# A two-iteration mixture stage: the state is kept as mu - x, and VectorE makes all picked rows

## What is computed

```python
v = zeros_like(xf); integrated = xf
for _ in range(2):
    ctx = concatenate([integrated, v], axis=-1)
    shared_ctrl = gelu(ctx @ shared_w1 + shared_b1) @ shared_w2 + shared_b2
    ctrl = experts(ctx, flat_idx, ...)            # two of eight experts a row, chosen once
    # for each of the three controls a, b, g = split(ctrl, 3):
    v_next = sigmoid(a) * v - softplus(b) * (x - mu)
    x_next = x + 0.1 * sigmoid(g) * v_next
    # weighted by sw, (1 - sw) * flat_w, and then by a halting share
    integrated = integrated + halt * (x_mix - integrated)
    v = v + halt * (v_mix - v)
refined = gelu(integrated @ refine_w1 + refine_b1) @ refine_w2 + refine_b2
out = xf + integration_weight * refined
```

## Time and profile before

| | |
|---|---|
| median of 3 runs | 3231.7 us (3231.43 to 3236.0) |
| the profiled execution | 3206.04 us |
| its span | 3204.3 us |
| PE busy | 2711.0 us (85%) |
| DVE busy | 2364.4 us (74%) |
| ACT busy | 1991.2 us (62%) |
| POOL busy | 1108.0 us (35%) |
| granted PE clock, mean | 0.897 |

### The profile page before, as it was taken

The page is one execution under the profiler, slowest core; times in us unless marked ns, Lnnn a source line. Parts: engine busy times, 40 slices in busy tenths (PEclk is TensorE's granted clock), DMA queues, the critical chain, the costliest instruction groups (busy, mean ns, idle before and its releaser), DMA issues. The chain is left out here.

```text
span 3204.3 us, 43614 instructions
## 1 busy us (share of the span) xinstructions
PE 2711.0 (85%) x16128; PEld 1864.2 (58%) x16128; DVE 2364.4 (74%) x3852; ACT 1991.2 (62%) x2961; POOL 1108.0 (35%) x824
## 2 busy tenths in 40 slices
PE   3989999898989907889888888988898889896986
PEld 2333333333333306777687767777786778685876
DVE  4577676677776736877887788778877887776998
ACT  1676676666667706666667666766676667664432
POOL 2112112021111114443445344434443444442776
PEclk8798898989899958989999899989898999898998
DMA  4352542516335030000000000000000000003231
GB/s 110 61 83 72 88 82 74 83 60 96 73 67 90 27 97 1 1 14 14 1 14 14 8 7 14 14 7 7 14 14 1 14 14 7 1 8 116 80 99 53
DMA packets 124789, 136.09 MB, mean 42 GB/s; under 512 B 16754, under 2 KB 104818, under 8 KB 124580
## 3 DMA queue, kind: packets, MB, share of 16 engines
q1 hardware_dynamic: 124580, 133.31, 18.4%
HBM read 86.87 MB, written 46.40 MB: 42 GB/s over the span
## 5 line engine op out<-in xcount | busy, mean ns | idle before, releaser
L380 ACT ACTIVATE probs<-psum_a 128x1024 f32<-128x1024 f32 (+3 forms) x768 | 604.3, 816 | 341.9 <-PE psum_a L643 337.9
L1410 PE MATMUL psum_f<-w,picked 128*128 128x256 f32 (+1 forms) x2304 | 722.4, 346 | 0.0
L1409 PE MATMUL psum_f<-w,picked 128*128 128x256 f32 x2304 | 626.3, 289 | 2.7 <-DVE picked L1238 2.7
L1410 PEld LDWEIGHTS psum_f<-w,picked 128*128 128x128 f32 x2304 | 452.2, 196 | 52.7
L975 POOL TENSOR_TENSOR picked<-hid,masks 128x512 fp32r<-128x512 f32 x256 | 347.0, 1365 | 368.7 <-PE psum_f L1410 326.5
L1409 PEld LDWEIGHTS psum_f<-w,picked 128*128 128x128 f32 x2304 | 456.7, 198 | 2.9 <-DVE picked L1238 2.9
L456 DVE TENSOR_SCALAR probs<-probs 128x2048 f32<-128x2048 f32 (+3 forms) x320 | 301.5, 942 | 192.4 <-ACT probs L380 192.4
L643 PE MATMUL psum_a<-q_stack,k_stack 72*128 72x512 f16 (+3 forms) x1536 | 399.3, 352 | 34.9 <-DMA q_stack<-q_rope_scratch 17.6
L1067 ACT ACTIVATE gates<-psum_f 128x256 f32<-128x256 f32 (+1 forms) x384 | 186.6, 492 | 302.4 <-PE psum_f L1410 278.7
L658 PE MATMUL psum_a<-probs,v 128*17 128x512 f32 (+3 forms) x3072 | 347.7, 527 | 1.8 <-DVE probs L456 1.7
L1238 DVE TENSOR_TENSOR picked<-hid,masks 128x512 fp32r<-128x512 f32 x256 | 228.6, 921 | 148.1 <-PE psum_f L1410 145.0
(11 more groups left out here) (284 smaller groups left out, 6096.2 us busy)
## 6 DMA issues: line engine op xcount, KB each, us to landing
heads_scratch<-kq_parts SPq DMA_DIRECT2D x64, 256.0 KB
k_stack<-heads_scratch SPq DMA_DIRECT2D x96, 128.0 KB
q_stack<-heads_scratch SPq DMA_DIRECT2D x96, 128.0 KB
x_in<-x_dram SPq DMA_DIRECT2D x8, 1024.0 KB, 5.3
x_res<-x_dram SPq DMA_DIRECT2D x16, 512.0 KB, 5.2
x_scratch<-y SPq DMA_DIRECT2D x16, 512.0 KB, 3.1
xs<-x_scratch SPq DMA_DIRECT2D x16, 512.0 KB, 3.9
xf_scratch<-xs SPq DMA_DIRECT2D x16, 512.0 KB, 2.9
```

The source lines that it names most:

```text
L380: act.activation(probs[:, s % PROB_SETS, 2 * u:2 * u + 2, q0:512], psum[:, 2 * u:2 * u + 2, q0:512], ACT.Exp, scale=exp_scale).then_inc(ex ...
L1409: pe.matmul(soft_out, x, cols[:, 1], start=start, stop=stop)
L1410: return pe.matmul(gate_out, x, cols[:, 2] if it == 0 else cols[:, 0::2], start=start, stop=stop)
```

## The change

1. The state in `xs` is mu - x from the normalisation on. `x_normalize` gets one more DVE operation over the block, x_minus_mu and its semaphore go from POOL, and `integrate` uses the state directly. The transposed state is negated where it is read out (ACT by a scale of -1, DVE by a multiplication by -1), and mu's share of each first layer, `W1^T mu`, is added to the biases once: 12 tiny matmuls and two additions at the start of `mixture`, 8 and one at the start of `refine`, with two more small loads of mu in each.
2. The iteration-0 update has 7 DVE instructions instead of 10; `tmp` gives way to `terms`, which holds both sums side by side.
3. The moments and the normalisation of a new block are made half a block earlier: behind the updates of units 2 and 3 of the "first" group of the block before.
4. DVE makes the lower picked rows as well (`pick`).
5. Of the ten mask spreads, DVE reads the five odd ones (`spread_rows`), ahead of its update of unit 2; and spread 1 goes from the fills of unit 1 to those of unit 2.

```diff
-                [("HT", k, 0, 0), ("H", k, 0, 0), ("H", k, 0, 1), ("MT", k, 0, 0), ("SP", k, 0, 0), ("SP", k, 0, 1)],
-                [("H", k, 0, 2)] + [("SP", k, 0, i) for i in range(2, 10)]]
+                [("HT", k, 0, 0), ("H", k, 0, 0), ("H", k, 0, 1), ("MT", k, 0, 0), ("SP", k, 0, 0)],
+                [("H", k, 0, 2)] + [("SP", k, 0, i) for i in range(1, 10)]]
...
     def on_act(job):
-        return job[0] in ("XT", "RT", "H", "LG", "HT") or job[0] == "SP"
+        return job[0] in ("XT", "RT", "H", "LG", "HT") or job[0] == "SP" and job[3] % 2 == 0
...
-            def pick_lower(n):
...
-            def x_minus_mu(n):
...
-                if t == 2 and kind == "second" and k + 2 < BLOCKS:
-                    x_scale(k + 2)
...
+                if t == 3 and kind == "first" and k + 1 < BLOCKS:
+                    x_scale(k + 1)
+                for job in hidden_jobs:
+                    lower_parts(job)
...
-                    act.activation(ctx_t[:, 0, i], src, ACT.Copy).then_inc(act_read, 1)
+                    act.activation(ctx_t[:, 0, i], src, ACT.Copy, scale=-1.0 if i < 2 else 1.0).then_inc(act_read, 1)
...
+            dve.wait_ge(mu_part, 1)
+            dve.tensor_tensor(b1[:], b1[:], psum[:, 0, 0:5], ALU.add)
+            after(dve.tensor_tensor(br1[:], br1[:], psum[0:HIDDEN, 0, 5:6], ALU.add))
...
-                last.then_inc(xn_ready, 1)
+                then_wait(last)
+                dve.tensor_tensor(xs[:, k % XS], mu[:].unsqueeze(1).to_broadcast([P, BT, D]), xs[:, k % XS],
+                                  ALU.subtract).then_inc(xn_ready, 1)
...
+            def spread_rows(k, places):
+
+                for i in places:
+                    job = ("SP", k, 0, i)
+                    job_ready(dve, job)
+                    s, place = divmod(i, 5)
+                    dve.tensor_copy(masks[:, k % MASKS, s, place], bank(job), saturate=False).then_inc(dve_read, 1)
...
                 for s in range(2):
                     if n >= 2:
                         dve.wait_ge(slot_done, SLOTS * (n - 2) + s + 2)
...
+                    for part, done in ((0, upper_picked), (1, lower_picked)):
+                        if (t, s, part) == (0, 0, 1):
+                            dve.wait_ge(lower_made, lower_value[("H", k, it, FULL - 1)])
+                        first = part if s == 0 else 1 - part
+                        dve.tensor_tensor(picked[:, n % 2, s, part], hid[:, hid_set(k, it), part, first:first + 4, tile_of(t)].bitcast(F32),
+                                          masks[:, k % MASKS, s, first:first + 4, tile_of(t)], ALU.mult).then_inc(done, 1)
...
                 if it == 0:
+                    then_wait(dve.tensor_tensor(q, sp_b, c.unsqueeze(2).to_broadcast([P, SLOTS, D]), ALU.mult))
+                    then_wait(dve.scalar_tensor_tensor(out=r, in0=tg, scalar=1.0, in1=q, op0=ALU.add, op1=ALU.mult))
                     for s in (1, 2):
+                        then_wait(dve.tensor_tensor(terms[:, 0], terms[:, 0], terms[:, s], ALU.add))
+                    dve.tensor_tensor(v, q[:, 0], z, ALU.mult)
+                    then_wait(dve.scalar_tensor_tensor(out=r[:, 0], in0=r[:, 0], scalar=-HALF_STEP, in1=z, op0=ALU.mult, op1=ALU.mult))
+                    dve.tensor_tensor(z, z, r[:, 0], ALU.add).then_inc(unit_done, 1)
...
+                if t == 2 and kind == "first":
+                    spread_rows(k, (1, 3, 5, 7, 9))
                 if t == 2:
                     integrate(n)
                 if n + 2 < UNITS:
-                    pick_upper(n + 2)
+                    pick(n + 2)
...
+                    if t == 2 and k + 1 < BLOCKS:
+                        x_row_stats(k + 1)
+                    if t == 3 and k + 1 < BLOCKS:
+                        x_normalize(k + 1)
                 if kind == "second":
                     if t == 1:
                         shared_lower(k, 1)
-                        if k + 2 < BLOCKS:
-                            x_row_stats(k + 2)
                     if t == 2:
                         coefficients(k, 1)
-                        if k + 2 < BLOCKS:
-                            x_normalize(k + 2)
...
+            pe.wait_ge(weights_in, 16 * len(loads))
+            for m in range(MC):
+                for c in range(2):
+                    last = pe.matmul(psum[:, 0, m:m + 1], raw_f1[:, c, P * m:P * m + P], mu_col[:, c:c + 1], start=(c == 0), stop=(c == 1))
```

More of the change, by code:

```diff
@@ L747, in on_act @@
     def on_act(job):
[L748 removed]
+        return job[0] in ("XT", "RT", "H", "LG", "HT") or job[0] == "SP" and job[3] % 2 == 0
     def on_dve(job):
[L751 removed]
+        return job[0] in ("XT", "MT") or job[0] == "SP" and job[3] % 2 == 1
     act_value = {job: n + 1 for n, job in enumerate([job for job in jobs if on_act(job)])}
@@ L1171, in x_lower @@
                 act_took(dve, job)
-                dve.tensor_tensor(ctx_t[:, 1, c], bank(job), ctx_t[:, 0, c].bitcast(F32), ALU.subtract).then_inc(dve_read, 1)
+                dve.scalar_tensor_tensor(out=ctx_t[:, 1, c], in0=bank(job), scalar=-1.0 if c < 2 else 1.0,
+                                         in1=ctx_t[:, 0, c].bitcast(F32), op0=ALU.mult, op1=ALU.subtract).then_inc(dve_read, 1)
             def shared_lower(k, it):
@@ L1274, in integrate @@
                     for s in range(SLOTS):
-                        last = dve.scalar_tensor_tensor(out=x, in0=tmp[:, s], scalar=d[s], in1=x, op0=ALU.mult, op1=ALU.add)
+                        last = dve.scalar_tensor_tensor(out=z, in0=q[:, s], scalar=d[s], in1=z, op0=ALU.mult, op1=ALU.add)
                         if s < SLOTS - 1:
@@ L1292, in _ @@
                 x_lower(1, 0, c)
-            pick_upper(0)
-            pick_upper(1)
+            pick(0)
+            pick(1)
             for n in range(UNITS):
@@ L1325, in _ @@
                         shared_lower(k, 1)
-                        if k + 2 < BLOCKS:
-                            x_row_stats(k + 2)
                     if t == 2:
                         coefficients(k, 1)
-                        if k + 2 < BLOCKS:
-                            x_normalize(k + 2)
         @block.tensor
         def _(pe):
+            pe.wait_ge(weights_in, 16 * len(loads))
+            for m in range(6):
+                for c in range(2):
+                    w = raw_w1[c][:, P * m:P * m + P] if m < 5 else raw_r1[:, c]
+                    last = pe.matmul(psum[0:w.shape[1], 0, m:m + 1], w, mu_col[:, c:c + 1], start=(c == 0), stop=(c == 1))
+            last.then_inc(mu_part, 1)
             pe.wait_ge(weights_ready, 1)
@@ L1522, in refine @@
                  (iw[:], W["integration_weight"].partition_broadcast(P))]
+        loads += [(mu_col[:, c:c + 1], W["mu"][P * c:P * c + P].unsqueeze(1)) for c in range(2)]
         loads += [(bf1[:, m:m + 1], W["refine_b1"][P * m:P * m + P].unsqueeze(1)) for m in range(MC)]
@@ L1587, in _ @@
                     job_ready(act, job)
-                    act.activation(ctx_t[:, k % 2, 0, i], bank(job), ACT.Copy).then_inc(act_read, 1)
+                    act.activation(ctx_t[:, k % 2, 0, i], bank(job), ACT.Copy, scale=-1.0).then_inc(act_read, 1)
                 if kind == "H":
```

89 lines of the change are left out of this document (27 added, 62 removed).

## The result

The changed kernel takes 3132.4 us (median of 4 runs, 3129.0 to 3148.9) beside 3231.6 us for the kernel before (median of 4): a ratio of 0.9701, with an interval of 0.9665 to 0.9736. The forecast was 3127 us. Medians and ranges in this document take in every execution, ratios and their intervals leave out those over 1.5% above the fastest of their kernel.

What follows compares the result with a forecast made beforehand. PE, which does most work, was taken to be held up where DVE is full. The terms, -92.5 - 13 - 16 + 13 + 3.5 + 1 = -104 us, from the median 3231.7 us gave 3127 us; range 3078 to 3200.

Steps and rivals of the forecast that it cites:

- -92.5 us for the wait: Mixture stage: PE's wait for the normalised rows before its transposes, 92.5 us in 14 places, goes.
- the walk: DVE's order of work through one mixture block: PE waits about 0.9 us for copies, 3 us in hand at picks.
- -13 us for the clock behind it: Transposes after the wait for the rows: the lower clock's penalty goes, 0.94 us times 14, 13 us.
- -16 us for spread 1: Early mask spread moved behind the third layer's job: 0.79 us gap gone, one matmul hidden, 1.1 us a block, 16 us.
- +13 us for late copies: First layer after the transposes: PE waits about 0.9 us for DVE's last copies, 14 times, 13 us lost.
- Ends, +3.5 and +1: First blocks: new subtraction and second normalisation, less collisions, cost 3.5 us; refine stage's small loads of mu cost 1 us.
- DVE's account: DVE's busy time in a steady mixture block: from 84.7 to 88.8 us, with 9.6 us back from fewer POOL collisions.
- (a): Iteration-0 half: DVE runs late, PE waits for copies or picks, some 4 us a block lost; 3183 us, chance 0.19.
- (b): Mixture blocks: DVE becomes the bound with 104.1 us of work, a block of 118.8 us; 3398 us, chance 0.07.
- (c): Unit 3 and slots after transposes: faster spreads keep PE's clock up, 3 us more a block; 3082 us, chance 0.12.
- (d): Before the transposes: another wait ends where the normalised rows did, so nothing visible changes; 3232 us, chance 0.06.
- The profiled time, 3102 us: Whole kernel's profiled execution: 3206.0 us, 25.7 us under the median, less 104 us gives 3102 us.

Runs made afterwards that it cites:

- e1: The kernel before with only the moments and normalisation moved half a block earlier; 3153.1 us, ratio 0.9712.
- e2: The changed kernel with moments and normalisation back in the iteration-0 half; 3175.7 us, ratio 0.9808.
- e6: The changed kernel plus 16 multiplications a block on POOL that nobody reads or waits for; 3218.6 us, ratio 0.9983.
- e4: The changed kernel with all ten mask spreads of a block copied by ScalarE; 3141.3 us, ratio 0.9711.
- e3: The changed kernel with the 16 lower picks of a block back on POOL; 3191.5 us, ratio 0.9864.
- e5: The kernel before with only the lower picks moved from POOL to DVE; 3184.2 us, ratio 0.9886.

## Why the prediction was right, point by point

- **What bounded the kernel: right.** PE was held up where DVE was full. The wait was gone in after and in e1, and came back, shortened, in e2.
- **-92.5 us for the wait: right.** -6.79 us a block against 92.5 / 14 = 6.6. Nothing else was late at that place: the walk had 3 us in hand at the picks, and the trace shows no wait there.
- **-13 us for the clock behind it: too small, by half.** The stretch from the transposes to the next `LG` shrank by 1.96 us a block, not 0.94. The prediction left the slots behind the transposes unpriced; they are the other 1.0 us, 14 us in all.
- **-16 us for spread 1: did not show.** Its 0.79 us wait is gone (the places in the list fell from 42 to 30), yet `LG` to the gap is not shorter (32.38 to 32.49). Block by block the two parts come apart. At the same clock behind `LG` the stretch is 1.0 us shorter, close to the forecast 1.1: 31.4 us before and 30.4 after at 1.00, 33.0 and 32.0 at 0.79. But the mean clock there went from 0.89 to 0.72, and that takes 1.1 us back. e1, in which the spread is not moved, has 33.22 us at 0.77, +0.84 by the clock alone. This step failed in its sum: it priced the clock behind the wait that goes, and not the clock behind the wait that stays. The matmul of the spread isn't hidden either, but stands behind the gap (+0.29). The miss cancelled the term above, -14 against +16: that the total came out so near is partly luck.
- **+13 us for late copies: right.** The walk had them end 61.3 us behind `LG` (2057.4 - 1996.08); they end 62.5 us behind it (1935.35 - 1872.84), and all of the difference is that DVE's last spread ends 36.2 us behind `LG` in this block, not 35.0. The wait itself is 0.42 us, half of the forecast 0.9. The stretch grew by 1.09 us all the same, since the matmuls in it run a little slower: those of the first layer start every 0.232 us there, where it was 0.228. Why, no run shows.
- **Ends, +3.5 and +1: right in size, not in parts.** From the first work of the mixture's prologue to the first transposes it is 59.9 us before and 63.4 after. The 1.2 us for the new subtraction are in it; the rest is 1.2 us of longer waiting for the loads (38.84 to 40.07), and about 1 us for clearing the larger `terms` and for the two additions. The 2.5 us for the second block's normalisation came too (its transposes are 27.3 us behind the first instead of 24.5), but inside the stage. `refine`, from DVE's start on, took 260.9 and 261.1 us.
- **DVE's account.** Forecast 88.8 us a block, measured 85.87. The signs that were named came in, or nearly: block 100.4 (98 to 100), POOL 16.9 (about 16), picks 0.72 us (near 0.65; a single free one is 0.68), under 1 us of idleness before the first-layer matmuls. The term that was off is the relief: 84.0 + 16 x 0.62 + 3.5 + 1.2 - 1.2 is 97.4, so DVE got back 11.5 us, where 9.6 were taken. Groups of DVE in 1340 to 2760 us show what collisions are left:
```profile
L1224 DVE TENSOR_TENSOR picked<-hid,masks 128x512 fp32r<-128x512 f32 x449 | 295.3, 716 | 21.5 <-PE psum_f L1402 19.4 <-POOL hid L965 1.2 <-ACT hid L1026 0.5
L1248 DVE TENSOR_TENSOR terms<-terms 128x512 f32<-128x512 f32 x114 | 118.9, 1043 | 3.9
L1254 DVE SCALAR_TENSOR_TENSOR terms<-gates,vs 128x768 f32<-128x768 f32 x56 | 68.7, 1226 | 0.0
L1246 DVE SCALAR_TENSOR_TENSOR terms<-gates,terms 128x768 f32<-128x768 f32 x57 | 67.3, 1181 | 2.0
L1255 DVE TENSOR_TENSOR terms<-terms,soft_b 128x768 f32<-128x768 f32 x56 | 67.2, 1201 | 1.9
```
Where POOL is idle, one such instruction takes 0.68, 0.69, 0.95, 0.96 and 0.96 us. The excess over that, times 32, 8, 4, 4 and 4 a block, is 6.8 us. Counted over all instructions of DVE in 13 blocks, each against the median of its kind where POOL is idle (over seven of the runs), it is 9.0 us for 11 POOL instructions: 0.8 each, the figure that the prediction took. The same count gives 20.6 us a block before and 17.3 in e6. So the 11.5 us that DVE got back by the change, and the 8.2 that it lost in e6, are both time in which its instructions ran longer beside POOL. The Trainium skill (SBUF — State Buffer, "SBUF: two separate sides") lets the second of the two engines block until the first is through; an estimate from it for ten lower parts of 1.4 to 1.6 us, each met at its start, is about 15 us. The trace agrees with the kind of blocking, and the cost, 0.8 us, is about half of a POOL instruction, as if DVE arrived in the middle of it on the mean:
```profile
1942.74 1.60 POOL L960 TENSOR_TENSOR hid<-gel,hid 64x512 fp32r<-64x512 f32 x1 [22.33 <-ACT hid L1024]
1944.42 1.89 POOL L962 TENSOR_TENSOR hid<-gel,hid 64x512 fp32r<-64x512 f32 x1
```
```profile
1943.23 1.93 DVE L1246 SCALAR_TENSOR_TENSOR terms<-gates,terms 128x768 f32<-128x768 f32 x1
1945.19 3.36 DVE L1248 TENSOR_TENSOR terms<-terms 128x512 f32<-128x512 f32 x2
```
  The DVE instruction of 1943.23 ends at 1945.16, 0.82 us behind the end of the POOL instruction that it met (1944.34), and its two successors take 1.68 us each where 0.71 is free.
- **The five spreads on DVE priced at nothing: right** (e4, 0.3 us).
- **The rivals.** (a), the wait moves, did not happen in after, but did in e1 (25.4 us), e3 (36.9 us) and e6 (50.1 us), the kernels in which POOL goes on beside it: it was POOL's silence that kept it away. (b) decides once DVE's work passes 92 us a block; e6 put it at 94.1 us, and lost 93.5 us of the stage. By the rule of (b) its block would be 94.1 + 14.7 = 108.8 us; it was 106.3, so DVE's idleness, 14.7 us in that rule, shrank to 12.3. (c) named the clock in the slots behind the transposes, and that half of it came true, -1.0 us a block, while its other half did not. (d) did not happen: no other wait ended where the one for the rows did.
- **The profiled time, 3102 us: wrong, 3132.6.** The prediction carried the 25.7 us by which the profiled execution of before was under its median over to after. The profile of after shows where they went: the attention stage, which the change doesn't touch, took 23.7 us longer in it (the mixture's first work at 1167.5 instead of 1143.7 us), at a mean granted clock of 0.86 instead of 0.89. So -100.9 for the stage, +3.5 and +0.2 for the ends and +23.7 make -73.5, and the spans differ by 73.4. Without the attention stage it is -97.2; the medians differ by 99.2; the sum of the forecast was -104.

## What to carry to other kernels

Count what one engine's instructions cost the others before asking how long they take: moving an operation onto the busier engine can relieve it, if the operation left behind blocked it from outside (in e5, 16 picks of 0.62 us went to DVE for 1.7 us of busy time). To find out beforehand, add idle work of the same shape to the engine in question and see what it costs. And when a wait is removed, price again the short waits that stay near it, since the clock behind them may be another afterwards; look at several blocks before you say which, as neighbouring blocks of one kernel can differ in it.

## What the runs showed of the hardware beyond what was expected

- Work on POOL that nobody needs and nobody waits for, 16 multiplications of 1.25 us in a block of 100 us, made the block 5.9 us longer (e6).
- Equal idleness of PE, different clocks: behind 1.65 us of idleness before `LG` the granted clock of the next 8 us was 1.00 in 6 blocks of the kernel before and 0.79 in 7, mostly in turn; behind 1.59 us it was 1.00 in one block of the kernel after and 0.79 or 0.57 in 12.
- The attention stage, the same code in all kernels, took 23.7 us longer in one profiled execution than in another, which is a quarter of what was to be measured. Over the ten profiled executions it took between 1138.0 us (e6) and 1188.8 us (e2), and on the whole the longer it took, the longer PE was at the lower level of its clock in it: 231 us in the shortest, 388 us in the longest, 247 before and 321 after. Why the clock differs there, no run shows. Stage lengths of the part that was changed were the sharper measure.
